# Re-ordering the stage from the last scores to the attention output in a one-core Perceiver layer

## The reference

```python
x = x + xattn(layernorm(x), ctx)        # ctx: 25088 rows
x = x + attn(layernorm(x))              # 16 heads of 64, masked
x = x + ffn(layernorm(x))               # shared expert + top-1 of 32 experts

# xattn (both directions are attentions; the second one is short)
c2s  = softmax((q_c @ k_s.T) * scale) @ v_s       # over the 25088 rows
s2c  = interp(softmax((q_s @ k_c.T) * scale) @ v_c)
gate = sigmoid(concat(c2s, s2c) @ Wg.T + bg)
out  = gate * c2s + (1 - gate) * s2c
# attn: q, k, v = x @ Wq + bq, ...; keys 0..127 for the first half of the queries, causal in the second
out  = softmax(mask(q @ k.T / 8)) @ v @ Wo
```

## Time and profile before

| | us |
|---|---|
| median of 3 runs (1190.36 to 1191.41) | 1190.37 |
| the profiled execution | 1193.42 |
| its span, first to last instruction | 1191.7 |
| end of the scores of the last block | 593.43 |
| start of pair 3's scores (first full turn of the head loop) | 694.66 |
| DVE takes the finished attention output | 725.09 |

### The profile page before, as it was taken

The page is one execution under the profiler, slowest core; times in us unless marked ns, Lnnn a source line. Parts: engine busy times, 40 slices in busy tenths (PEclk is TensorE's granted clock), DMA queues, the critical chain, the costliest instruction groups (busy, mean ns, idle before and its releaser), DMA issues.

```text
span 1191.7 us, 17007 instructions
## 1 busy us (share of the span) xinstructions
PE 1057.2 (89%) x6822; PEld 721.9 (61%) x6822; DVE 615.5 (52%) x980; ACT 373.1 (31%) x546; POOL 3.5 (0%) x20
## 2 busy tenths in 40 slices
PE   8999999999999999999999999999886666666666
PEld 8867888888888888888766756555332222222223
DVE  4457888788788788788743265323121111111111
ACT  2444465465465455455432163100000000000000
POOL 1000000000000000000000000000000000000000
PEclk9999999999999999999999989999998989988899
DMA  9448899887787787787739216999999999999996
GB/s 345 178 142 303 305 351 334 299 310 265 274 300 273 268 297 269 278 295 270 278 118 405 82 61 248 424 427 425 427 427 424 429 428 427 429 427 428 430 425 280
DMA packets 90722, 381.49 MB, mean 320 GB/s; under 512 B 5568, under 2 KB 5696, under 8 KB 73792
## 3 DMA queue, kind: packets, MB, share of 16 engines
q1 hardware_dynamic: 90688, 381.00, 82.6%
HBM read 355.29 MB, written 25.69 MB: 320 GB/s over the span
## 4 chain that ended last, share of the span: by engine, by line
PE 68%; DMA 28%; DVE 2%; ACT 1%; issue 0%; SPq 0%; DVEq 0%
DMA wd<-in_r_down 22%; PE ps L537 7%; PE ps L535 7%; PE ps L536 7%; PE ps L550 7%; PE ps L549 7%; PE ps L548 7%; DMA wu<-in_r_up 4%; PE ps L905 4%; PE ps L840 2%; PE ps L508 2%; PE ps L521 2%; PE ps L894 2%; PE ps L921 1%; PE ps L888 1%; PE ps L728 1%
## 5 line engine op out<-in xcount | busy, mean ns | idle before, releaser
L535 PE MATMUL ps<-ctt_hi,q_hi 128*128 128x512 f32 x392 | 155.8, 397 | 0.0
L537 PE MATMUL ps<-ctt_hi,q_lo 128*128 128x512 f32 x392 | 154.6, 394 | 0.0
L536 PE MATMUL ps<-ctt_lo,q_hi 128*128 128x512 f32 x392 | 154.6, 394 | 0.0
L550 PE MATMUL ps<-nat_hi,pt_lo 128*128 128x512 f32 x368 | 145.5, 395 | 0.0
L548 PE MATMUL ps<-nat_hi,pt_hi 128*128 128x512 f32 x368 | 144.9, 394 | 0.7 <-DVE pt_lo L1183 0.7
L549 PE MATMUL ps<-nat_lo,pt_hi 128*128 128x512 f32 x368 | 145.2, 394 | 0.0
L1125 ACT ACTIVATE sg<-ps 128x256 f32<-128x256 f32 x32 | 12.3, 385 | 407.5 <-PE ps L888 407.5
L1510 DVE TENSOR_TENSOR hh<-sg,ps 128x256 f32<-128x256 f32 x32 | 13.5, 421 | 232.8 <-PE ps L894 232.8
L905 PE MATMUL ps<-wd,hh_t 128*32 128x512 f32 x512 | 78.1, 737 | 56.0 <-DMA wd<-in_r_down 56.0
L1173 DVE TENSOR_TENSOR ctt_lo<-ctt,ctt_hi 128x2048 fp32r<-128x2048 f32 x49 | 111.0, 2290 | 20.5 <-ACT ctt_hi L964 20.4
L968 ACT ACTIVATE nat_hi<-nat 128x2048 fp32r<-128x2048 f32 x48 | 92.0, 1917 | 83.5 <-DMA nat<-in_ctx_rows 83.5
(11 more groups left out here) (274 smaller groups left out, 1315.4 us busy)
## 6 DMA issues: line engine op xcount, KB each, us to landing
wu<-in_r_up SPq DMA_DIRECT2D x32, 2048.0 KB, 27.4
wd<-in_r_down SPq DMA_DIRECT2D x32, 2048.0 KB, 25.9
wg<-in_r_gate SPq DMA_DIRECT2D x30, 2048.0 KB, 26.0
ctt<-in_ctx_t SPq DMA_DIRECT2D x49, 1024.0 KB, 7.9
nat<-in_ctx_rows SPq DMA_DIRECT2D x48, 1024.0 KB, 7.3
strips<-turned SPq DMA_DIRECT2D x96, 256.0 KB, 5.7
pt<-strips SPq DMA_DIRECT2D x24, 1024.0 KB, 4.8
w_gate<-in_w_g_t SPq DMA_DIRECT2D x2, 1024.0 KB, 13.7
```

Source lines behind the costliest of these rows:

```text
L535: mm(o, qh, ctt_hi[par][:, c, :], start=(c == 0), stop=False)
L536: mm(o, qh, ctt_lo[par][:, c, :], start=False, stop=False)
L537: last = mm(o, ql, ctt_hi[par][:, c, :], start=False, stop=(c == HC - 1))
L550: last = mm(o, p_lo[:, w, :], n_hi[:, t, :], start=False, stop=(final and t == KT - 1))
```

## The change

The same matmuls, activations and vector operations are issued in another order, with these differences in what is issued:

- The `s2c` half of the gate is split (`gate2_part`). Tile 0's four matmuls stay where they were. Two of tile 1's come between `c2s_transposes(1)` and `gate1_tile(1)`, and the last two behind the transposes of tile 0's `an`. The signal `gate1_in_psum` is renamed `gate_in_psum`.
- `end_transposes` moves behind `first_block(0)`; both tiles' `first_block` come first; `acc_transposes`, `c2s_tile` and `c2s_transposes` are interleaved anew. ACT makes both halves of `pt_hi` before the last block's exponentials. DVE makes `end_nat_lo` before `end_pt_lo`.
- The three `keep_warm` calls are gone.
- Query chunks 4 to 7 use 256 columns in one matmul (16 matmuls) where there were two of 128 (32 matmuls).
- `pair_scores(0)` comes after keys 0 to 5, keys 6 and 7 after it, then `pair_scores(1)`, two heads' transposes, the first half of tile 1's values, `pair_scores(2)`, two more heads' transposes, `pair_products(0)`, the second half of tile 1's values. The loop over pairs starts at c = 2. DVE's `key_columns` and `value_rows` are put among `head_norm` and `head_max` to suit. PSUM banks of values and keys change.

```diff
+
+            def gate2_part(t, cs):
+                for c in cs:
+                    last = mm(ps[:, 2 + t, :], s2c_t[:, c, t * P:(t + 1) * P], w_gate2[:, c, :],
+                              start=(c == 0), stop=(t == 1 and c == HC - 1))
+                return last
...
-                    last = mm(ps[:, 2 + t, :], c2s_t[:, c, t * P:(t + 1) * P], w_gate1[:, c, :], start=False, stop=(c == HC - 1))
-                last.then_inc(s["gate1_in_psum"], 1)
-
+                    last = mm(ps[:, 2 + t, :], c2s_t[:, c, t * P:(t + 1) * P], w_gate1[:, c, :],
+                              start=False, stop=(t == 0 and c == HC - 1))
+                return last
+
+            gate2_part(0, range(HC))
             pe.wait_ge(s["acc_ready"], NS)
             first_block(0)
+            end_transposes()
+            first_block(1)
             second_block(0)
             last_block(0)
-            first_block(1)
+            second_block(1)
             acc_transposes(0)
-            second_block(1)
+            last_block(1)
             c2s_tile(0)
-            last_block(1)
+            acc_transposes(1)
             c2s_transposes(0)
-            acc_transposes(1)
-            gate1_tile(0)
             c2s_tile(1)
-            keep_warm(14, 0)
+            gate1_tile(0).then_inc(s["gate_in_psum"], 1)
             c2s_transposes(1)
+            gate2_part(1, range(HC // 2))
             gate1_tile(1)
...
-            v_bank = [6, 7, 2, 3]
-            k_bank = [0, 0, 1, 1, 6, 6, 7, 7]
-
-            def values(t):
-                for n in range(2):
-                    for c in range(HC):
-                        last = mm(ps[:, v_bank[2 * t + n], :], a_t[:, c, t * P:(t + 1) * P], w_v[:, c, n * D:(n + 1) * D],
-                                  start=(c == 0), stop=(c == HC - 1))
-                    last.then_inc(s["va_in_psum"], 1)
-
             transpose_tile(0, an, s["an_ready"], s["at_in_psum"])
-            keep_warm(12, 1)
-            pe.wait_ge(s["at_ready"], 1)
-            pe.wait_ge(s["watt_loaded"], 96)
-            values(0)
-            pe.wait_ge(s["z_ready"], 2)
-            project_tile(0, by_chunk(2, AC), w_q, a_t, range(AC))
-            transpose_tile(1, an, s["an_ready"], s["at_in_psum"])
-            keep_warm(8, 0)
...
-            project_tile(1, by_chunk(2, AC), w_q, a_t, range(AC), s["qa_in_psum"])
...
-            for o in range(AC):
+            gate2_part(1, range(HC // 2, HC)).then_inc(s["gate_in_psum"], 1)
...
+            v_bank = [6, 7, 3, 5]
+            k_bank = [0, 0, 1, 1, 4, 4, 5, 5]
+
+            def values(t, n):
+                for c in range(HC):
+                    last = mm(ps[:, v_bank[2 * t + n], :], a_t[:, c, t * P:(t + 1) * P], w_v[:, c, n * D:(n + 1) * D],
+                              start=(c == 0), stop=(c == HC - 1))
+                last.then_inc(s["va_in_psum"], 1)
+
+            def keys(o):
...
+            pe.wait_ge(s["at_ready"], 1)
+            pe.wait_ge(s["watt_loaded"], 96)
+            for n in range(2):
+                values(0, n)
+            transpose_tile(1, an, s["an_ready"], s["at_in_psum"])
+            pe.wait_ge(s["z_ready"], 2)
+            project_tile(0, by_chunk(2, AC), w_q, a_t, range(AC // 2))
+            pe.wait_ge(s["at_ready"], 2)
+            project_tile(1, by_chunk(2, AC), w_q, a_t, range(AC // 2), s["qa_in_psum"])
+            for o in range(AC // 2, AC):
+                for c in range(HC):
+                    last = mm(by_chunk(2, AC)[:, o, :], w_q[:, c, o * P:(o + 1) * P], a_t[:, c, :],
+                              start=(c == 0), stop=(c == HC - 1))
+                last.then_inc(s["qa_in_psum"], 1)
+            for o in range(4):
+                keys(o)
             pe.wait_ge(s["qa_ready"], AC)
-            values(1)
+            for o in range(4, 6):
+                keys(o)
...
+            pe.wait_ge(s["va_ready"], 2)
+            pe.wait_ge(s["ka_ready"], 1)
+            pair_scores(0)
+            for o in range(6, AC):
+                keys(o)
+            pe.wait_ge(s["ka_ready"], 2)
+            pair_scores(1)
+            for h in range(2):
+                head_transposes(h)
+            values(1, 0)
             pe.wait_ge(s["ka_ready"], AC)
-            pe.wait_ge(s["va_ready"], 1)
-            pair_scores(0)
+            pair_scores(2)
+            for h in range(2, 4):
+                head_transposes(h)
+            pe.wait_ge(s["va_ready"], 3)
+            pair_products(0)
+            values(1, 1)
             pe.wait_ge(s["va_ready"], 4)
             pe.wait_ge(s["wo_loaded"], 16)
-            for c in range(AC):
+            for c in range(2, AC):
                 if c + 1 < AC:
                     pair_scores(c + 1)
                 head_transposes(2 * c)
-                if c >= 2:
-                    output_part(c - 2, 0)
+                output_part(c - 2, 0)
                 head_transposes(2 * c + 1)
-                if c >= 1:
-                    pair_products(c - 1)
-                if c >= 2:
-                    output_part(c - 2, 1)
+                pair_products(c - 1)
+                output_part(c - 2, 1)
...
+            act.wait_ge(s["products_done"], NB - 3)
+            for half in range(2):
+                probs_hi(NS - 1, half)
             exps(NS, 0, halves=1)
-            probs_hi(NS - 1, 0)
-            act.wait_ge(s["products_done"], NB - 3)
-            probs_hi(NS - 1, 1)
...
             acc_columns(0)
+            acc_columns(1)
             c2s_columns(0)
-            acc_columns(1)
             gate_tile(0)
+            c2s_columns(1)
             deviation(2, 0, 1)
-            c2s_columns(1)
+            a_columns(0)
             gate_tile(1)
-            a_columns(0)
             deviation(3, 1, 2)
             a_columns(1)
...
+            rows_lo(NB - 1, end_nat, end_nat_hi, end_nat_lo)
...
-            rows_lo(NB - 1, end_nat, end_nat_hi, end_nat_lo)
...
-            v_bank = [6, 7, 2, 3]
-            k_bank = [0, 0, 1, 1, 6, 6, 7, 7]
+            v_bank = [6, 7, 3, 5]
+            k_bank = [0, 0, 1, 1, 4, 4, 5, 5]
 
             add_pair(0)
             add_last(0)
             add_pair(1)
+            add_last(1)
             c2s_out(0)
-            add_last(1)
             difference(0)
+            c2s_out(1)
             gated(0)
-            layernorm(2, an, s["an_ready"], 0, 1, meanwhile=lambda: c2s_out(1))
+            layernorm(2, an, s["an_ready"], 0, 1)
             difference(1)
             gated(1)
             layernorm(3, an, s["an_ready"], 1, 2)
             value_rows(0)
...
-            for o in range(AC):
+
+            def key_columns(o):
...
-            value_rows(2)
-            value_rows(3)
...
+            for o in range(6):
+                key_columns(o)
             for h in range(2):
                 head_max(h)
             for c in range(AC):
                 for h in range(2 * c, 2 * c + 2):
                     head_norm(h)
+                if c == 0:
+                    for o in range(6, AC):
+                        key_columns(o)
                 for h in range(2 * c + 2, min(2 * c + 4, NH)):
                     head_max(h)
+                if c < 2:
+                    value_rows(2 + c)
```

More of the change, by code:

```diff
@@ L240, in perceiver_layer @@
         turned_ready end_pt_in_psum pt_hi_ready pt_lo_ready products_done end_products acc_ready
-        acct_in_psum acct_ready c2s_in_psum c2s_ready c2st_in_psum c2st_ready gate1_in_psum z_ready
+        acct_in_psum acct_ready c2s_in_psum c2s_ready c2st_in_psum c2st_ready gate_in_psum z_ready
         gate_ready an_ready at_in_psum at_ready qa_in_psum qa_ready ka_in_psum ka_ready
@@ L392, in _ @@
             sp.dma_start(flat(wg[0]), runs(a["s_gate"])).then_inc(gw_loaded[0], 16)
-            sp.wait_ge(s["gate1_in_psum"], QT)
+            sp.wait_ge(s["gate_in_psum"], QT)
             sp.dma_start(flat(wu[0]), runs(a["s_up"])).then_inc(uw_loaded[0], 16)
@@ L648, in _ @@
             pe.wait_ge(s["exp_ready"], NB - 1)
-            for t in range(QT):
-                for c in range(HC):
-                    mm(ps[:, 2 + t, :], s2c_t[:, c, t * P:(t + 1) * P], w_gate2[:, c, :], start=(c == 0), stop=False)
-            end_transposes()
+            def gate2_part(t, cs):
[3 more added lines that the diff above has]
+                return last
             def tile_products(b, q, acc_bank, p_hi, p_lo, n_hi, n_lo, first, final):
@@ L732, in _ @@
-            transpose_tile(0, an, s["an_ready"], s["at_in_psum"])
-            keep_warm(12, 1)
-            pe.wait_ge(s["at_ready"], 1)
-            pe.wait_ge(s["watt_loaded"], 96)
-            values(0)
-            pe.wait_ge(s["z_ready"], 2)
-            project_tile(0, by_chunk(2, AC), w_q, a_t, range(AC))
-            transpose_tile(1, an, s["an_ready"], s["at_in_psum"])
-            keep_warm(8, 0)
-            pe.wait_ge(s["at_ready"], 2)
-            project_tile(1, by_chunk(2, AC), w_q, a_t, range(AC), s["qa_in_psum"])
@@ L743, in _ @@
```

(7 more changed lines are left out.)

## The result

The change makes the kernel faster: 1186.07 us (median of 6 executions, 1184.21 to 1187.66) beside 1190.99 for the kernel before on the same chip (median of 6, 1190.36 to 1194.04). The recorded ratio is 0.9949, 95% interval 0.9936 to 0.9962: 6.1 us less, between 4.5 and 7.6. It is not the quotient of the two medians, which are 4.9 us apart, and it is the figure that comes with an interval. The forecast was 1181.4 in 1179.3 to 1186.5; the sign and the range held, and the point lies 4.7 us too low. The profiled execution took 1187.66, span 1185.8.

The account below looks back on a forecast made before the run. Loading bounds the last third, which starts at the attention output; PE bounds the stage before. 13.2 us lost plus 0.5 on queries less 4.6 of new waits, called 9.0: 1190.37 - 9.0 = 1181.4, range 1179.3 to 1186.5.

Parts of the forecast that it names:

- The end follows the attention output: Expert weight stream after the middle stage: the end is attention output plus a constant, so each microsecond before counts fully.
- DVE as bound: Rival, chance 0.08: key and value copies among the norms make the head start lose 6.8 again; gain 4.5, time 1185.9.
- 13.2 us lost before: PE in the old middle stage: 6.4 us lost up to the first head scores plus 6.8 at the head start.
- Wait 1: PE before the first products, waiting for `pt_lo`: 1.2 us, bounds 1.1 to 2.4.
- Waits 2 and 3: PE before `c2s_transposes(0)`, 0.6 us, and before `gate1_tile(1)` and the transposes of `an`, 0.5 in all.
- Wait 5: First two heads' softmax, hidden behind keys 6 and 7 and second scores: costs nothing; without those keys 3.45 us.
- Waits 6 and 7: PE at heads 2 and 3 (0.75 and 0.5 us) and before `pair_scores(3)` (1.0): 2.25, bounds 0 to 6.8.
- No fall of the clock: PE in the stage: granted clock stays 1.00 up to pair 3's scores, as the longest new wait is 1.2 us.
- one fall: Rival, chance 0.15: PE's clock falls once around the heads, costing 3.35 us; gain 5.7, time 1184.7.
- two falls: Rival, chance 0.04: clock falls at the first new wait and at the heads; gain 2.3, time 1188.1.
- a long half clock: Rival, chance 0.03: PE stays at 1.2 GHz through gate, values and queries; slower, 1194.4 at 26 us.
- The table load: ACT before `an`: a function change costs 1.3 us by the trace, 2.66 by the skill page, then gain 7.9.

Follow-up runs that it names:

- e7_spacer: Changed kernel with 150 small idle matmuls put between the first gate half and the first products; 1192.75 us, ratio 0.999 to the kernel before.
- e2_after: Changed kernel, unedited, profiled and timed a second time; 1184.26 us, ratio 0.9921 to the kernel before.
- e10_exps: Changed kernel with ACT's old order for the last blocks, the exponentials ahead of `pt_hi`; 1186.65 us, ratio 0.9949 to the kernel before.
- e9_bare: Changed kernel with keys 6 and 7 put back in front of `pair_scores(0)`; 1189.6 us, ratio 0.9964 to the kernel before.
- e12_wait: Second run of the same kernel as e6_wait; 1184.55 us, ratio 0.993 to the kernel before.
- e11_after: Changed kernel, unedited, a third time; 1186.1 us, ratio 0.9949 to the kernel before.
- e6_wait: Changed kernel with DVE's value copies behind the norms and PE waiting for the last only before `output_part(0, 1)`; 1184.64 us, ratio 0.9916 to the kernel before.
- e1_before: Kernel before, unedited, profiled and timed once more; 1191.78 us, ratio 0.9995.
- e8_cold: Kernel before without its three `keep_warm` calls, nothing else changed; 1195.85 us, ratio 1.0011.
- e3_front: Changed kernel with the new order only up to the queries; keys, values and heads as in the kernel before; 1186.91 us, ratio 0.9956.
- e4_heads: Changed kernel with the old order and keep-warm up to the queries, the new order from the keys on; 1191.24 us, ratio 0.9975.

## Why the prediction was right, and what it mis-sized

- *The end follows the attention output.* Right, and tested by e7_spacer. One row under it was misread: the plateau of the earlier trace rows begins with the 26th slice, at 745 us; the 25th, at 715 us, still has 248 GB/s. And the middle stage does not load little on the whole, since its first 89 us move 207 GB/s. Neither changes the sum.
- *The range.* It held with some luck. The mechanism's own range was 1179.3 to 1183, and 1186.07 lies outside it, next to the 1185.9 of "DVE as bound". By the time alone that rival would look right. The traces exclude it, and the distance comes from outside the stage, as told below.
- *13.2 us lost before.* The place and most of the size were right: both halves give it back, 4.6 and 4.8 us taken alone.
- *Queries.* 7.14 + 6.91 = 14.05, as forecast.
- *Wait 1, 1.2 us.* Mis-sized. PE finishes the gate half at 594.93 + 3.44 and starts the products at 600.01: 1.64; e2_after 1.38. `pt` took 4.8 to land as in the earlier trace rows, ACT 1.06 and DVE 1.24. But the issue stood only 2.22 us ahead of the gate half where it was 2.54 before. What sets this wait is how the load's issue falls against the last scores, and that moves by some tenths. The upper bound, 2.4, is what e10_exps met (2.41 of recorded idle) without the new ACT order: that reorder is worth 1.0 directly.
- *Waits 2 and 3, 0.6 and 0.5.* 0.41 and 0.19 as recorded idle. Counted as wait 1 was, from the end of the work by its pitch to the next start, they are 0.57 (621.95 to 622.52) and 0.39 (635.47 to 635.86): right.
- *The front in all.* The work up to pair 0 is 83.0 less the query gain of 0.5 and less the 10.3 moved behind it, 72.2. The window is 75.07, so 2.9 are lost, against a forecast of 1.2 + 0.6 + 0.5 = 2.3. Of the 0.6, 0.4 are wait 1; the rest is in small pieces that show no idle.
- *Wait 5, "without the keys it would cost those 3.45".* e9_bare cost 3.6, but by another sum: 1.9 of idle and 1.6 to 1.7 of low clock. The number is right by luck.
- *Waits 6 and 7, 2.25.* Right: 17.69 less 15.39 of work (three scores 2.94, four transposes 1.32, a product 0.81, keys 3.45, values 6.87) is 2.3. Inside it wait 6 was 1.0 (1.25 forecast) and wait 7 1.04 (1.0); the last 0.3 is in small pieces.
- *No fall of the clock.* Right in the stage, in all three profiles of after; one fall was the first rival, and e10_exps and e9_bare show how near it was: waits of 2.41 and 1.90 us brought it back, at 1.6 us of extra time, where I had priced a fall at 3.35. The reason that I gave, a longest wait of 1.2 us against 1.9, is not enough by itself. In after's own loop PE waits 1.98 us at full clock, as the last section shows.
- *DVE as bound, two falls, a long half clock.* Not seen.
- *The table load.* The square root's load starts at 631.94 and the activation at 634.05, released by the variance and not by the load. The Trainium skill, "ScalarE: Activation LUTs", section "What ACT_TABLE_LOAD costs", adds a drain to the load, 2.66 us in all; as an estimate from that page the activation could not have started before 634.60. The trace does not agree with it here either: 2.11 us lie between the two starts, and only 1.90 between those of tile 1's sigmoid (637.26 and 639.16). The 1.3 us of the earlier trace rows stand.

ACT's timeline, after:

```profile
631.94 1.28 ACT L982 ACT_TABLE_LOAD   x1
634.05 0.20 ACT L982 ACTIVATE st<-st 128x1 f32<-128x1 f32 x1 [0.83 <-DVE st L1178]
```

What was off is the last step: "1190.37 - 9.0". The stage gave 8.5 to 8.65, so the mechanism was sized within 0.5. But I put the whole difference of two stages onto a median, as though loop and tail were the same in every execution. The loop ranged from 591.6 to 598.8 and the tail from 466.5 to 468.0 over the profiles. Most of the loop's spread is shown, by the 0 to 3.6 us of `pt_lo` waits and the low clock of the first 18 us, and what sets either is not. The tail is 1.1 to 1.5 longer in after, e10_exps and e12_wait, not in e2_after, e11_after or e6_wait, the first two of which have after's code. In after and e12_wait the chain that ended last goes, in its tail, through loads of the up weights, where the earlier trace rows has the down weights; in e10_exps it ends in down weights as before, so this turn is not the whole reason:

```profile
1143.58 27.39 DMA wu<-in_r_up
```

Why some executions have the longer tail is open. None of the three profiles with the old order throughout (before, e1_before, e8_cold) has it, but three are too few to say that the change has no part in it. Open, too, is whether the 6.1 us of the first comparison and the 9.4 of e2_after differ by more than that spread; the stage says 8.65 and lies between them.

## What to carry to other kernels

When a change touches one stage, cut the profile at the stage's own events and compare stages; these repeated within 0.25 us here while the gains in whole time of the same code differed by 3 us. Price a forecast of the whole with the spread of the parts that are not touched. A wait costs its own length and, for some of those from 1.7 us up here, a fall of the clock on top: cover the longest waits first with matmuls that are needed anyway, and if a copy stands on the critical engine ahead of what PE wants next, move it behind, as e6_wait did for 2.0 us.

## What the runs showed of the hardware that was not expected

A single gap on PE could bring the granted clock to 0.50 (1.2 GHz). In the stage, each gap of 1.90 us (before, e1_before, e3_front, e8_cold, e9_bare) and the one of 2.41 (e10_exps) had it behind it, and gaps up to 1.49 (after) and 1.53 (e8_cold) passed at 1.00.

The length of the gap does not decide alone. In the loop of after, a gap of 1.98 us passed at 1.00, and so did one of 1.79 in e12_wait. At the first weight load, gaps of 1.68 (e4_heads), 1.79 (e11_after) and 2.02 (e6_wait) were followed by 0.50, and one of 1.65 (e1_before) was not. PE's timeline and window of after, then of e6_wait:

```profile
243.76 0.47 PE L548 MATMUL ps<-nat_hi,pt_hi 128*128 128x512 f32 x1 [1.98 <-DVE pt_lo L1206]
...
243.76:248.00 4.24, 4.24 (x18) 3.46 (x19) 4.10 (x8) 3.15 (x4) 0.00 (x0) 1.00 1.05 395
```

```profile
10.16 3.75 PE L508 MATMUL ps<-c_t,w_qc 128*128 128x128 f32 x16 [2.02 <-DMA w_qc<-in_w_qc_t]
...
10.10:16.00 5.90, 5.84 (x27) 5.87 (x28) 1.13 (x4) 0.00 (x0) 0.00 (x0) 0.50 1.02 364
```

What else decides is open. In the stage the clock was still 1.00 in the gap and fell within 2 us of its end, so it was the work behind that paid: 3.2 us in e9_bare and 3.6 in e10_exps with PE busy throughout, 6.7 in before (5.31 busy) and 9.5 in e8_cold (8.12 busy). The long ones have a second gap, of 1.38 or 1.39 us, behind the first, but e6_wait's 5.9 us at the start have none, so that the second gap prolongs the fall is not shown.
